# Third stage of a two-layer decoder: sink added by TensorE, exponent's argument as score minus maximum, cosine product kept in PSUM

## What is computed

```python
x = x + _L1_attn_ref(_layernorm(x), wq, wk, wv, wo, sink)     # part D
x = x + _L1_xattn_ref(_layernorm(x), ctx, ctx, ...)           # part E
x = x + _L1_ffn_ref(_layernorm(x), ...)                       # parts F and M

# part D
q = rope(x @ wq); k = rope(x @ wk); v = x @ wv
att = einsum('bhqd,bhkd->bhqk', q, k) * 16 ** -0.5 + sink     # sink: one number per head
att = softmax(att)                                            # a sequence lies inside the window
out = einsum('bhqk,bhkd->bqhd', att, v) @ wo
```

## Time and profile before

| | |
|---|---|
| median of 3 runs | 3060.1 us |
| the profiled execution | 3064.77 us, span 3063.0 us |
| third stage | from 1937 us to the end of the span |
| VectorE busy, whole span | 2565.5 us (84%) |
| TensorE busy, whole span | 2760.3 us (90%) |
| GpSimd busy, whole span | 2126.1 us (69%) |
| ScalarE busy, whole span | 1954.2 us (64%) |
| mean granted clock of TensorE | 0.951 |

### The profile page before, as it was taken

How to read it: one execution, slowest core, us unless ns; L and a number is a source line. 1 busy time by engine, 2 the same in 40 slices (tenths; PEclk the granted TensorE clock), 3 DMA queues, 4 the chain that set the end, 5 groups by cost and what they waited for, 6 DMA issues and landing times. The chain is left out here.

```text
span 3063.0 us, 68267 instructions
## 1 busy us (share of the span) xinstructions
PE 2760.3 (90%) x22128; PEld 2307.7 (75%) x22128; DVE 2565.5 (84%) x5547; ACT 1954.2 (64%) x4120; POOL 2126.1 (69%) x2651
## 2 busy tenths in 40 slices
PE   6999999999999999999788499558899999999978
PEld 3888888888888888888455399436777777777767
DVE  6888888888888888888499577488999999999973
ACT  5888778788787878878344155345656565565642
POOL 5897666666666666666378455288888888888870
PEclk9999999999999999999899699768999999999999
DMA  4564344444344444443444599300000000000000
GB/s 144 172 206 161 130 151 130 149 133 150 128 130 145 142 138 142 147 138 112 139 152 145 190 334 336 132 14 19 17 27 19 27 19 25 21 24 22 20 5 11
DMA packets 186021, 340.09 MB, mean 111 GB/s; under 512 B 40810, under 2 KB 104179, under 8 KB 179075
## 3 DMA queue, kind: packets, MB, share of 16 engines
q1 hardware_dynamic: 179586, 319.55, 31.8%
q0 software_dynamic: 6144, 16.79, 1.8%
HBM read 264.67 MB, written 63.18 MB: 107 GB/s over the span
## 5 line engine op out<-in xcount | busy, mean ns | idle before, releaser
L1802 POOL TENSOR_TENSOR l_prod<-l_sco,l_kv 128x256 f32<-128x256 f32 x512 | 380.4, 783 | 43.3 <-DVE l_sco L2316 43.3
L1795 POOL TENSOR_TENSOR l_prod<-l_q,l_kv 128x256 f32<-128x256 f32 x512 | 358.6, 742 | 57.8 <-DVE l_att L2324 57.8
L718 DVE SCALAR_TENSOR_TENSOR a_cq<-a_PQ,a_taps,a_cq 128x504 f32<-128x504 f32 (+2 forms) x384 | 281.8, 734 | 75.9 <-ACT a_cq L584 66.8
L718 DVE SCALAR_TENSOR_TENSOR a_ck<-a_PK,a_taps,a_ck 128x504 f32<-128x504 f32 (+2 forms) x384 | 280.7, 731 | 9.6 <-ACT a_ck L584 0.3
L342 POOL TENSOR_TENSOR a_tq<-a_cq,a_tq 128x512 f32<-128x512 f32 x128 | 166.0, 1297 | 130.8 <-ACT a_tq L590 130.4
L329 POOL TENSOR_TENSOR a_hrs<-a_hve,a_neghalf 128x8 f32<-128x8 f32 x128 | 209.7, 1638 | 25.2 <-DVE a_hve L735 25.2
L485 PE MATMUL a_Y<-a_wo,a_og_parts 128*128 128x256 f32 x1536 | 207.2, 285 | 4.5 <-POOL a_og_parts L336 4.5
L412 PEld LDWEIGHTS a_X<-a_wv,a_xb 128*128 128x128 f32 x1536 | 199.9, 188 | 12.1 <-issue 1.2
L412 PE MATMUL a_PQ<-a_x_hi,a_wqk 128*128 (+1 forms) x512 | 196.2, 424 | 12.6 <-issue 11.9
L342 POOL TENSOR_TENSOR a_tk<-a_ck,a_tk 128x512 f32<-128x512 f32 x128 | 163.7, 1279 | 62.6 <-ACT a_tk L590 62.6
L412 PE MATMUL a_X<-a_wv,a_xb 128*128 128x256 f32 x1536 | 204.1, 282 | 0.8 <-DMA a_xb<-a_x_lo 0.8
(11 more groups left out here) (400 smaller groups left out, 8488.7 us busy)
## 6 DMA issues: line engine op xcount, KB each, us to landing
a_wqk<-qk_parts SPq DMA_DIRECT2D x112, 512.0 KB, 3.3
m_wgu<-gate_up_parts SPq DMA_DIRECT2D x39, 1024.0 KB, 7.5
a_wv<-v_parts SPq DMA_DIRECT2D x56, 512.0 KB, 3.7
a_wg<-g_parts SPq DMA_DIRECT2D x112, 256.0 KB, 3.3
a_wo<-o_parts SPq DMA_DIRECT2D x112, 256.0 KB, 2.9
a_dr<-decays SPq DMA_DIRECT2D x256, 64.0 KB, 2.5
m_hs<-sorted_rows SPq DMA_DIRECT2D x39, 256.0 KB, 6.5
sorted_outs<-m_ys SPq DMA_DIRECT2D x39, 256.0 KB, 6.8
```

The costliest lines, as they stand in the source:

```text
L718: nc.vector.scalar_tensor_tensor(out=acc, in0=src, scalar=taps[p][:, tap + k:tap + k + 1], in1=acc, op0=ALU.mult, op1=ALU.add).then_inc(s_ ...
L1795: nc.gpsimd.tensor_tensor(out=prod[:, h], in0=qv[:, h:h + 1, :].to_broadcast([P, H, HD]), in1=kk, op=ALU.mult).then_inc(S("E_pqk"), 1)
L1802: nc.gpsimd.tensor_tensor(out=prod[:, h], in0=sco[:, h:h + 1, :].to_broadcast([P, HD, H]), in1=vv, op=ALU.mult).then_inc(S("E_pav"), 1)
```

## The change

Four edits, all but the last in the third stage.

1. The sink is no longer added by VectorE. The second stage splits it, repeated 64 times per head and beside the biases it split before, into three bf16 pieces and writes them to the DRAM table `bias_rows`; the third stage loads them as `sink3` (3 x 1024), in place of a 128 x 16 load, as the last of the same six transfers. TensorE opens D's two score banks with a product of three rows, `inverse3` (1/SC everywhere) times 512 columns of `sink3`, where an identity times two columns stood; the score products now add to it.
2. The maximum is subtracted before scaling: VectorE writes score minus maximum, and ScalarE's exponential multiplies by SC. The small steps L2266, L2269 (D) and L2271 (F) are gone, and the large step is a tensor_tensor in place of a scalar_tensor_tensor.
3. In the rotary step the sine product comes first, the cosine product waits for it and writes back into P0, and the additions read one input from P0 and one from SBUF. P0 is free for the next piece after the additions, where it was free after the products.
4. The buffers for the biases are 16 columns wide in place of 8, and `hm` and `qr` shrink or go. One more constant is set at the start of the third stage.

```diff
-            "P0": [("d_qk", "D", [("D_rt", 2, 2)]), ...
+            "P0": [("d_qk", "D", [("D_qk", 2, 2)]), ...
...
-            for tensor, name in ((dwqk, "dwqk"), (rope, "rope"), (sink, "sink"), (headmask, "headmask"), (dwv, "dwv"), (dwo, "dwo")):
+            for tensor, name in ((dwqk, "dwqk"), (rope, "rope"), (headmask, "headmask"), (dwv, "dwv"), (dwo, "dwo")):
                 sp.dma_start(tensor[:], a[name]).then_inc(S("d_in"), 16)
+            sp.dma_start(sink3[:].rearrange("q b n -> q (b n)"), bias_rows[:, 4 * D:4 * D + H * SEQ]).then_inc(S("d_in"), 16)
...
-                        nc.tensor.matmul(SS[:, half, 0:2], identb[:], identb[:, 0:2], start=True, stop=False, skip_group_check=True)
+                        nc.tensor.matmul(SS[:, half, :], inverse3[:], sink3[:, half, :], start=True, stop=False, skip_group_check=True)
...
-                                                    start=k == "D" and c == 0, stop=True, skip_group_check=True)
+                                                    start=False, stop=True, skip_group_check=True)
...
-                    nc.scalar.activation(ex[k][:], ex[k][:], ACT.Exp).then_inc(S(k + "_exp"), 1)
+                    nc.scalar.activation(ex[k][:], ex[k][:], ACT.Exp, scale=SC).then_inc(S(k + "_exp"), 1)
...
+                qr = P0[:, 0:QKD].rearrange("p (h d) -> p h d", d=HD)
-                nc.vector.tensor_tensor(out=qr[:], in0=P0[:, 0:QKD].rearrange("p (h d) -> p h d", d=HD), in1=cos,
-                                        op=ALU.mult).then_inc(S("D_rt"), 1)
                 nc.vector.tensor_tensor(out=rt[:].rearrange("p h (f j) -> p h f j", f=2), in0=x[:, :, ::-1, :],
                                         in1=sin.rearrange("p h (f j) -> p h f j", f=2), op=ALU.mult).then_inc(S("D_rt"), 1)
+                dve.wait_ge(S("D_rt"), 2 * t + 1)
+                nc.vector.tensor_tensor(out=qr, in0=qr, in1=cos, op=ALU.mult).then_inc(S("D_rt"), 1)
                 dve.wait_ge(S("D_rt"), 2 * t + 2)
...
-                    nc.vector.reduce_max(hm[k][:, 0, :], ss, axis=AX).then_inc(S(k + "_max"), 1)
+                    nc.vector.reduce_max(hm[k][:], ss, axis=AX).then_inc(S(k + "_max"), 1)
+                    wait_if(dve, S(k + "_eTp"), t)
                     dve.wait_ge(S(k + "_max"), t + 1)
-                    if k == "D":
-                        nc.vector.scalar_tensor_tensor(out=hm[k][:, 1, :], in0=hm[k][:, 0, :], scalar=SC, in1=sink[:], op0=ALU.mult,
-                                                       op1=ALU.add).then_inc(S("D_top"), 1)
-                        dve.wait_ge(S("D_top"), t + 1)
-                        nc.vector.tensor_tensor(out=hm[k][:, 2, :], in0=sink[:], in1=hm[k][:, 1, :], op=ALU.subtract).then_inc(S("D_shift"), 1)
-                    else:
-                        nc.vector.tensor_scalar(hm[k][:, 2, :], hm[k][:, 0, :], -SC, None, ALU.mult).then_inc(S("F_shift"), 1)
-                    wait_if(dve, S(k + "_eTp"), t)
-                    dve.wait_ge(S(k + "_shift"), t + 1)
-                    nc.vector.scalar_tensor_tensor(out=ex[k][:], in0=ss, scalar=SC, in1=hm[k][:, 2, :].unsqueeze(2).to_broadcast([P, H, SEQ]),
-                                                   op0=ALU.mult, op1=ALU.add).then_inc(S(k + "_arg"), 1)
+                    nc.vector.tensor_tensor(out=ex[k][:], in0=ss, in1=hm[k][:].unsqueeze(2).to_broadcast([P, H, SEQ]),
+                                            op=ALU.subtract).then_inc(S(k + "_arg"), 1)
...
+            nc.vector.memset(inverse3[:], 1.0 / SC).then_inc(S("const"), 1)
...
-        bias_rows = nc.dram_tensor("bias_rows", (3, 4 * D), BF16, kind="Internal").ap()
+        bias_rows = nc.dram_tensor("bias_rows", (3, 4 * D + 16 * SEQ), BF16, kind="Internal").ap()
```

More of the change, by code:

```diff
@@ L811, in recurrence_and_experts @@
         wd_high, wd_low = sb("wd_high", [P, E, DC, D], F32R), sb("wd_low", [P, E, DC, D], F32R)
-        b_in, b_rest = sb("b_in", [P, 8]), sb("b_rest", [P, 8])
-        b_piece = some(3, "b_piece", [P, 8], BF16)
+        b_in, b_rest = sb("b_in", [P, 16]), sb("b_rest", [P, 16])
+        b_piece = some(3, "b_piece", [P, 16], BF16)
         wkv, bkv, kvs = sb("wkv", [P, DC, 2 * D]), sb("bkv", [3, 2 * D], BF16), some(2, "kvs", [P, 2 * D])
@@ L1649, in layer_one @@
         dwqk, dwv, dwo = sb("dwqk", [P, DC, QKD]), sb("dwv", [P, DC, 64]), sb("dwo", [P, DC, D])
-        rope, sink = sb("rope", [P, 2, HD]), sb("sink", [P, H])
+        rope = sb("rope", [P, 2, HD])
+        sink3, inverse3 = sb("sink3", [3, 2, BLK], BF16), sb("inverse3", [3, P], BF16)
         ewq, ewo = sb("ewq", [P, DC, D]), sb("ewo", [P, DC, D])
@@ L2031, in _ @@
             pe.wait_ge(S("d_in"), 16 * D_WEIGHTS)
-            pe.wait_ge(S("const"), 12)
+            pe.wait_ge(S("const"), 13)
             pe.wait_ge(S("masked"), 4)
```

16 lines of the change are left out of this document (8 added, 8 removed).

## The result

The changed kernel takes 3035.15 us (median of 4 runs, 3033.89 to 3037.18), against 3063.57 us for the kernel before (4 runs, 3059.43 to 3067.85): a ratio of 0.9906, 95% interval 0.989 to 0.9922. It is faster by 28 us. The forecast was 3031 us in a range of 3003 to 3056, with a saving of 29 us from a median of 3060.1; a fourth run of the kernel before has since moved that median up by 3.5 us, and most of the 4 us between forecast and result is that. The profiled execution took 3033.89 us (span 3032.2, mean clock 0.956), 30.9 us less than the profiled one of before.

What follows compares the result with a forecast made beforehand. VectorE's list was taken as the bound, with TensorE's path capping the gain: 1.00 us over 27 rounds plus 2 us for F's last tiles, 29 us off a median of 3060.1, giving 3031 us, range 3003 to 3056.

Steps and rivals of the forecast that it cites:

- VectorE's list: VectorE's steps of a third-stage round, without a gap, taken as the bound; the change takes 2.56 us from it.
- TensorE's path: Closed path from F's maximum over L2363 and TensorE's 19.49 us to F's next maximum; 0.90 us of slack.
- The new round of 30.17: Round on TensorE's path after the change: 10.01 on VectorE, 0.14, 19.49 + 0.39 on TensorE, 0.14.
- F's arguments: VectorE after F's maximum: small step L2271 goes, saving 0.42 us in this round, 0.55 over all rounds.
- The sink's 0.39: TensorE opening D's banks with two products of 512 columns instead of 2: 0.39 us more a round.
- A, TensorE's path gives way: Rival: the next path decides, GpSimd's at 29.30 us a round, 3010 us; chance 0.16, including 0.03 for VectorE alone.
- D's arguments, 1.22: VectorE after D's maximum: L2266 and L2269 go, so the large step starts 1.22 us earlier.
- The rotary step, 0.79: VectorE's rotary step falls from 2.67 to 1.88 us as the additions read one input from PSUM.
- D, the rival in which the additions stay slow: Rotary additions stay at 0.95 us, step 2.94, result 3036 us; counted within the main forecast's 0.60.
- 27 rounds of 1.00, and 2 us: Total saving: 1.00 us in each of 27 rounds, plus 2 us from F's last four tiles; 29 us together.
- B, the clock: Rival: half-clock spells on TensorE cost up to 1.9 us each, leaving 3048 or up to 3084 us; slower 0.10.
- C, other steps wait longer for GpSimd: Rival: one VectorE wait of 2.4 us each round, round 30.95, 3055 us; with many clock spells 0.14.

Runs made afterwards that it cites:

- d_steps_back: Changed kernel with two small VectorE steps, results unused, put back between D's maximum and the large step; 3035.52 us.
- double_open: Changed kernel with the pair of TensorE products that opens D's score banks issued twice; 3047.1 us.
- f_step_back: Changed kernel with one small VectorE step, result unused, put back between F's maximum and the large step; 3052.61 us.
- only_rope: Kernel before with the changed rotary step alone; 3036.3 us.
- no_sink: Changed kernel with the sink added nowhere, D's score banks opened by two columns of an identity again; 3028.62 us.
- no_sink_root: Changed kernel with the sink added nowhere and F's root on GpSimd moved ahead of the gather; 3024.18 us.
- rope_back: Changed kernel with the rotary step as before (products into SBUF, both additions from SBUF); 3050.56 us.
- after_root: Changed kernel with F's root on GpSimd moved ahead of the gather and nothing else; 3036.74 us.
- only_D: Kernel before with the sink added by TensorE and D's two small steps gone, F's small step and rotary step as before; 3060.74 us.
- rope_back_root: Changed kernel with the rotary step as before and F's root on GpSimd moved ahead of the gather; 3037.52 us.
- only_F: Kernel before with F's small step gone, the scale inside the exponential, and nothing else; 3051.8 us.

## Why the prediction was right, point by point

**VectorE's list was the bound, and TensorE's path is the next.** Right. The round fell to the sum of that path, and it was shown from three sides: 1.35 us taken from VectorE's spare time cost nothing (d_steps_back), 0.44 on TensorE cost 0.44 (double_open), a step of 0.55 between F's maximum and L2358 cost 0.55 (f_step_back). What the prediction did not see is that a second path lies 0.1 us under it.

**The new round of 30.17.** Measured 29.98. VectorE's term was 10.09 against 10.01: the large step of F starts 0.11 us behind the end of the maximum, not 0.04, so F's arguments saved 0.34 and not 0.42. TensorE's term was 19.61 against 19.88. The sink's 0.39 was right (2418.24 - 2417.71 = 0.53 for the pair, against 0.13); what the sum had not taken off is some 0.27 us of pauses inside the old 19.49 which hung on VectorE and went as VectorE came earlier: without the sink the term is 19.21 to 19.23 in only_rope, no_sink and no_sink_root. The rows show where. F's opening pair started at 2437.54, 0.14 us behind the end of D's large step (2436.17 + 1.23), so it waited for VectorE, and D's value projection waited for D's residual:

```profile
2427.60 0.41 DVE L2293 TENSOR_TENSOR x_sb<-l_EB,x_sb 128x256 f32<-128x256 f32 x1
2428.07 0.66 PE L1840 MATMUL l_EB<-l_dwv,l_xTD 128*128 128x64 f32 x4
```

From the start of the path to D's opening pair pass 10.89 us before and 10.72 after; the other 0.1 is F's pair. "With hardly a pause" was the wrong reading of the earlier trace rows, and "its pauses in those 19.49 us are not all TensorE's own" under A the right one.

**D's arguments, 1.22.** The large step of D now starts 1.31 us after the maximum does, and VectorE waits instead. Part of the sum of 2.56 for VectorE's list, worth nothing by itself, as the prediction had it.

**The rotary step, 0.79.** From 2407.56 to 2409.28 it takes 1.72 us against 2.67 before, a saving of 0.95; the prediction had 1.88. The additions came out at 424 and 412 ns against the 418 and 425 of the earlier trace rows. By the Trainium skill (SBUF — State Buffer, SBUF: two separate sides) a VectorE instruction with two SBUF inputs and a GpSimd instruction that reads SBUF lock each other out for a whole instruction; the fall from 946 to 424 with one input moved to PSUM agrees with it, and so does the return to 939 in rope_back. The cosine product, costed at 0.48 within 0.42 and 0.96, took 499 ns, 17 more than the sine product; the 65 ns more for PSUM by the Trainium skill (Perfetto Trace Analysis, Optimizing Scalar/DVE Operations) show in none of these rows. D, the rival in which the additions stay slow, fell.

**27 rounds of 1.00, and 2 us.** Rounds 4 to 27 sum to 748.3 us before and 720.9 after, a gain of 27.4 over 24 rounds (1.14 each, part of it from the clock spells that went). The first three rounds gave 3.3, the last four cost 0.5 in place of giving 2. The total came out right in part by luck. The first 27 rounds gave 30.7 where 27 were forecast and the last four 0.5 less than nothing where 2 were. Also, 0.21 of each 1.00 is the distance from the mean round (31.17) to the undisturbed one (30.96): the sum set a mean of before against an undisturbed round of after, and so took the clock spells in that mean as gone, without a reason of its own. They did go.

**A, TensorE's path gives way.** It did not. But its price was wrong: "GpSimd's path would then be 29.30" took the products alone. The path that runs on through the gather and F's root to F's transposes was not read, and with the sink left out it holds the round at 29.8 (3028 us). In the changed kernel it lies only 0.1 us under the round: had TensorE's path given way, the time would have stayed above 3030 by that sum (27 x 0.1 us under 3035, an estimate), and 3010 was not to be had.

**B, the clock.** The spells became rarer, as the price "against it" had it: the pause ahead of E's query projection is 0.75 us (1.45), and the clock from 2160 on is 1.00. The pause was expected to fall to 0.3. D's division (it ends at 2404.75 + 0.42 = 2405.17 in the round shown) does come 1.10 us earlier after F's scores of the round before (8.55 us against 9.65), but TensorE, too, reaches the projection 0.40 us earlier (7.95 us after the same scores against 8.35), which was not counted. What a spell costs was set too high: 1.2 us in f_step_back (31.77 against 30.53), where up to 1.9 were forecast.

**C, other steps wait longer for GpSimd.** Not in the full rounds of the changed kernel: L2221 takes 799 ns on average and L2341, which was L2346, 447. Near the end L2341 took 2.84 us once, as L2346 had before:

```profile
2923.23 2.77 POOL L1804 TENSOR_TENSOR l_prod<-l_sco,l_kv 128x256 f32<-128x256 f32 x4
2923.43 2.84 DVE L2341 TENSOR_TENSOR l_x<-l_x2f,l_x 128x256 fp32r<-128x256 f32 x1
```

Here, too, it ended behind the last product of the series, 0.27 us after 2923.23 + 2.77 = 2926.00. The bound of one product, 0.69 us, that the prediction set for such a wait does not hold: it was four products here and eight in after_root, where a round became 6 us longer. In only_D a wait did eat a gain: F's small step went from 448 to 614 ns.

**Which part brings the gain.** The prediction summed all parts for the list and then capped them by the path. That gives the right total and hides the shares: the rotary step alone gives 3036 us. By the steps of the prediction it alone was worth 0.79 x 27 = 21 us. It gave 27.6: the step saved 0.95, the sum of the gathered rows 0.1, and all but one of the clock spells between 2200 and 2880 us went.

## What to carry to other kernels

When the bound engine has only a little slack to the next closed path, price the change on that path, as the sum over the engine's list cannot come back; and list all closed paths, those through slow side engines and across two rounds too, since the next one may lie 0.2 us away. Parts that are each worth time alone may be worth nothing together, so measure each alone and each put back. A VectorE step with two SBUF inputs beside a busy GpSimd was worth moving to PSUM here for that alone (946 to 424 ns).

## What the runs showed of the hardware

- A product of three rows by 512 columns costs TensorE as much as one of 128 rows: the sink's pair takes 0.53 us, F's mask pair 0.52.
- The additions of the rotary step slowed GpSimd as well: its 16 value products take 12.00 us with them in SBUF, 11.62 with one input in PSUM, and 12.02 in rope_back_root, which has them in SBUF again.
- Small VectorE steps have no fixed price beside GpSimd. The step for F of 128x16 took 448 ns on average before, 346 in only_rope, 614 in only_D and 501 in f_step_back. What differs is where in a product of GpSimd it starts: in the rounds looked at it ends 0.03 us or so behind that product. From only_D and f_step_back:

```profile
2411.03 0.73 POOL L1797 TENSOR_TENSOR l_prod<-l_q,l_kv 128x256 f32<-128x256 f32 x1
2411.10 0.70 DVE L2269 TENSOR_SCALAR l_hmF<-l_hmF 128x16 f32<-128x16 f32 x1
...
2405.52 0.73 POOL L1798 TENSOR_TENSOR l_prod<-l_q,l_kv 128x256 f32<-128x256 f32 x1
2405.79 0.49 DVE L2271 TENSOR_SCALAR l_spare<-l_hmF 128x16 f32<-128x16 f32 x1
```

- TensorE's granted clock from 2160 us on goes with the pause ahead of E's query projection. It is 0.98 before, with 31.7 / 22 = 1.44 us of pause a round; 0.99 in only_D (1.41), f_step_back (1.34) and only_F (1.16); and 1.00 to two digits in only_rope (1.11) and in all kernels with less (changed kernel 0.77). In only_rope one spell is left, from 2704 us on, in a round whose pause was 1.46; the longest round of after_root has one behind a wait of 2.5. The rounds do not decide: double_open has rounds of 30.42 with a clock of 1.00, f_step_back rounds of 30.5 with spells. That the pause is the cause was not tried by itself.
